# Three stacked attention layers of a graph network: in the first two, the mean squares of odd node groups move from TensorE to ScalarE and VectorE

## What is computed

```python
h, _ = jax.lax.scan(layer, x, (W, att_src, att_dst, W_e, att_edge, bias, ln_gamma, ln_beta))   # 3 layers

def layer(h_in, p):
    Wl, asl, adl, Wel, ael, bl, gl, bel = p
    h = h_in @ Wl
    a = (h @ asl)[src_f] + (h @ adl)[dst_f] + ea_f @ (Wel @ ael)
    a = jnp.where(a > 0, a, 0.2 * a)
    m = jax.ops.segment_max(a, dst_f, num_segments=n)
    ea = jnp.exp(a - m[dst_f])
    denom = jax.ops.segment_sum(ea, dst_f, num_segments=n)
    alpha = ea / denom[dst_f]
    out = jax.ops.segment_sum(h[src_f] * alpha[:, None], dst_f, num_segments=n) + bl
    mu = jnp.mean(out, axis=-1, keepdims=True)
    var = jnp.var(out, axis=-1, keepdims=True)
    out = (out - mu) * jax.lax.rsqrt(var + 1e-05) * gl + bel
    return (out, None)
```

## Time and profile before

| | us |
|---|---|
| median of 3 runs (3552.34 to 3566.22) | 3566.04 |
| the profiled execution's own time | 3538.57 |
| its span, first to last instruction | 3536.8 |
| layer 0: first transposes to last weights matmul | 2020.9 to 2433.5 |
| layer 1: the same | 2445.6 to 2858.7 |
| layer 2: first transposes to the end of the span | 2872.5 to 3536.8 |

### The profile page before, as it was taken

How to read it: one execution, slowest core, us unless ns; L and a number is a source line. 1 busy time by engine, 2 the same in 40 slices (tenths; PEclk the granted TensorE clock), 3 DMA queues, 4 the chain that set the end, 5 groups by cost and what they waited for, 6 DMA issues and landing times. The chain is left out here.

```text
span 3536.8 us, 70121 instructions
## 1 busy us (share of the span) xinstructions
PE 2946.6 (83%) x18625; PEld 2422.4 (68%) x18625; DVE 2677.1 (76%) x8976; ACT 2360.3 (67%) x6177; POOL 2132.9 (60%) x2195
## 2 busy tenths in 40 slices
PE   5997899969886997988466599997999978888893
PEld 3776777755553554545366599997999878788883
DVE  5997999985443885999677548776588778889994
ACT  3997898962322565788466567775587657877994
POOL 7777777737775774776377477403772047721677
PEclk9998999988997998999788898788999777876555
DMA  4768865445553554455477589766898568975552
GB/s 125 219 220 134 170 171 183 168 142 163 170 165 105 141 154 131 140 182 175 141 230 234 188 284 288 225 198 190 268 289 254 178 194 269 282 237 180 160 167 84
DMA packets 429483, 671.96 MB, mean 190 GB/s; under 512 B 80739, under 2 KB 167414, under 8 KB 429196
## 3 DMA queue, kind: packets, MB, share of 16 engines
q1 hardware_dynamic: 354764, 558.83, 50.2%
q0 software_dynamic: 69408, 107.46, 12.8%
q10 hardware_dynamic: 5024, 2.30, 0.3%
HBM read 376.96 MB, written 295.31 MB: 190 GB/s over the span
## 5 line engine op out<-in xcount | busy, mean ns | idle before, releaser
L662 POOL DMA_INDIRECT msgs<-t_gat,row_i x591 | 571.3, 967 | 572.4 <-POOLq L158 388.6
L2244 ACT ACTIVATE t_nnt<-t_p_nt,cxt 128x512 f32<-128x512 f32 x294 | 201.0, 684 | 307.6 <-PE t_p_nt L2124 305.1
L1769 PEld LDWEIGHTS t_p_q<-mean_col,t_nsq 128*128 128x128 f32 x2352 | 353.4, 230 | 6.4 <-issue 6.4
L1769 PE MATMUL t_p_q<-mean_col,t_nsq 128*128 128x1 f32 x2352 | 339.0, 265 | 4.5 <-ACT t_asd L2270 3.9
L2038 POOL DMA_INDIRECT out_rows<-t_x,own_i x197 | 201.4, 1022 | 209.6 <-ACT t_x L2294 154.4
L2124 PE MATMUL t_p_nt<-ident,t_nh 128*128 128x128 f32 x1176 | 223.7, 323 | 78.7 <-DMA t_nh<-t_gat 67.1
L654 POOL DMA_INDIRECT rg_ring<-t_x,row_i x197 | 197.7, 1004 | 106.0 <-issue 51.9
L654 POOL DMA_INDIRECT gc_ring<-t_x,row_i x197 | 191.1, 970 | 116.6 <-issue 59.8
L1762 PE MATMUL t_p_nh<-wx,t_nnt 128*128 128x132 f32 x1568 | 259.5, 316 | 1.2 <-DVE t_nhn L1783 1.1
L679 POOL DMA_INDIRECT dg_g_ring<-in_x,dst_i x197 | 189.9, 964 | 110.4 <-DVE g_xb L1237 55.8
L654 POOL DMA_INDIRECT g_ring<-t_h,row_i x197 | 193.9, 984 | 85.3 <-issue 59.1
(11 more groups left out here) (407 smaller groups left out, 8612.0 us busy)
## 6 DMA issues: line engine op xcount, KB each, us to landing
t_nh<-t_gat SPq DMA_DIRECT2D x294, 264.0 KB
t_gat<-t_nhn SPq DMA_DIRECT2D x196, 264.0 KB
t_x<-de_x SPq DMA_DIRECT2D x196, 256.0 KB
t_ah<-t_gat SPq DMA_DIRECT2D x150, 264.0 KB
t_x<-t_x SPq DMA_DIRECT2D x148, 256.0 KB, 4.0
t_gat<-t_ahn SPq DMA_DIRECT2D x100, 264.0 KB
t_gat<-de_h SPq DMA_DIRECT2D x98, 264.0 KB
de_x<-in_x SPq DMA_DIRECT2D x97, 256.0 KB
```

Source lines behind the costliest of these rows:

```text
L662: self.nc.gpsimd.indirect_dma_start(out=self.msgs[:, c, 0:width], out_offset=None, in_=table, in_offset=bass.IndirectOffsetOnAxis(ap=idx[: ...
L1769: last = self.nc.tensor.matmul(p_q[:, j:j + 1], sq[:, j * D:(j + 1) * D], self.mean_col[:], start=True, stop=True)
L2244: nc.scalar.activation(nnt[:, g % 2], p_nt[:], ACT.Identity, bias=bias).then_inc(act_nt, 1)
```

## The change

In layers 0 and 1, odd node groups get their mean squares in another way. ACT squares the rows as they were loaded (`nh`, 128 of the 132 columns), DVE sums the squares along a row to four numbers for each partition (`nss`) and adds a fourth extra column that the table's rows now carry, and ACT takes the root with a bias. That column is twice the product of the row with the constant `cx`, so that the square of the sum of both comes out; `cx` squared goes into the root's bias (`shift2`). The column costs no instruction in the loop, since rows were 132 wide before; filling it and `shift2` takes five more DVE instructions in the program's first phase. The four one-column matmuls (eight instructions) of an odd group go, and its ACT square of `p_nt`, in whose place stands the square of the rows at the end of the tick's node steps. Even groups, all sum groups and layer 2 keep their steps. One semaphore for all roots becomes two, one for nodes and one for sums.

SP may load over an odd group's buffer only when DVE has added the extra column. PE may turn a group over an odd group's bank when ACT has copied it, with no square to wait for.

The plan's `node_time` goes from 2.6 to 2.3, which moves the weights to later ticks: batch 0 from tick 37 to 42, batch 1 from 60 to 66, batch 2 from 83 to 91. The table grows from 116 to 124 ticks. Node groups take ticks 0 to 101 in both. Sum groups start at ticks 45, 69 and 92 before, and at 50, 75 and 100 now. Ticks in which PE has node and sum steps: 40 before (45 to 60, 69 to 84, 92 to 99), 32 now (50 to 65, 75 to 90).

```diff
-PLAN = BATCHES, (96, 190, 290), 2.6, 2.6
+PLAN = BATCHES, (96, 190, 290), 2.3, 2.6
...
+            nc.vector.scalar_tensor_tensor(out=prod[:, 0], in0=self.wx[:, :, 0:D], scalar=2.0, in1=self.cx[:, :, 0:D],
+                                           op0=ALU.mult, op1=ALU.mult).then_inc(crossed, 1)
+            nc.vector.scalar_tensor_tensor(out=prod[:, 1], in0=self.cx[:, :, 0:D], scalar=1.0 / D, in1=self.cx[:, :, 0:D],
+                                           op0=ALU.mult, op1=ALU.mult).then_inc(crossed, 1)
+            dve.wait_ge(crossed, 2)
+            nc.vector.tensor_reduce(self.wx[:, :, D + 3], prod[:, 0], AXX, ALU.add).then_inc(crossed, 1)
+            nc.vector.tensor_reduce(self.shift2[:], prod[:, 1], AXX, ALU.add).then_inc(crossed, 1)
+            dve.wait_ge(crossed, 4)
+            nc.vector.tensor_scalar(self.shift2[:], self.shift2[:], EPS, None, ALU.add).then_inc(crossed, 1)
...
+            by_rows = lambda g: not last_layer and g % 2 == 1
...
                 def nodes(i):
                     if i < DG:
                         wait(sp, pe_nt, i - UN + 1)
+                        if by_rows(i - UN):
+                            wait(sp, dve_nss, squares(i - UN, True))
                         sp.dma_start(nh[:, i % UN], self.nodes(self.th[layer], 0, i)).then_inc(narr[i % UN], 16)
...
                         pe.wait_ge(narr[g % UN], 16 * (g // UN + 1))
-                        wait(pe, act_nq, g)
+                        wait(pe, act_nt, g)
+                        if not by_rows(g - 1):
+                            wait(pe, act_nq, g)
...
-                        pe.wait_ge(act_nq, g + 1)
-                        wait(pe, act_sd, roots["n", g] - 1)
-                        self.mean_squares(p_q, nsq[:, g % 2]).then_inc(pe_nq, 1)
+                        if not by_rows(g):
+                            pe.wait_ge(act_nq, g + 1)
+                            roots_taken(pe, "n", g)
+                            self.mean_squares(p_q, nsq[:, g % 2]).then_inc(pe_nq, 1)
...
-                        nc.scalar.activation(nsq[:, g % 2], p_nt[:], ACT.Square, bias=bias).then_inc(act_nq, 1)
+                        if not by_rows(g):
+                            nc.scalar.activation(nsq[:, g % 2], p_nt[:], ACT.Square, bias=bias).then_inc(act_nq, 1)
                     if 0 <= i - 2 < DG:
                         g = i - 2
-                        act.wait_ge(pe_nq, g + 1)
                         wait(act, dve_ninv, g - 1)
-                        nc.scalar.activation(nsd[:, g % 2], p_q[:, 0:G4], ACT.Sqrt, bias=self.eps[:]).then_inc(act_sd, 1)
+                        if not by_rows(g):
+                            act.wait_ge(pe_nq, squares(g, False))
+                            nc.scalar.activation(nsd[:, g % 2], p_q[:, 0:G4], ACT.Sqrt, bias=self.eps[:]).then_inc(act_nsd, 1)
+                        else:
+                            act.wait_ge(dve_nss, squares(g, True))
+                            nc.scalar.activation(nsd[:, g % 2], nss[:, g % 2], ACT.Sqrt, bias=self.shift2[:, layer:layer + 1],
+                                                 scale=1.0 / D).then_inc(act_nsd, 1)
+                    if 0 <= i - 1 < DG and by_rows(i - 1):
+                        g = i - 1
+                        act.wait_ge(narr[g % UN], 16 * (g // UN + 1))
+                        wait(act, dve_ns, squares(g - 2, True))
+                        nc.scalar.activation(rows_of(nsq[:, g % 2]), nh[:, g % UN, :, 0:D], ACT.Square).then_inc(act_nq, 1)
...
                         self.gat_rows_out(nhn[:, g % 3], p_nh, ninv[:, g % 2]).then_inc(dve_nhn, 1)
+                    if 0 <= i - 1 < DG and by_rows(i - 1):
+                        g = i - 1
+                        dve.wait_ge(act_nq, g + 1)
+                        wait(dve, act_nsd, g - 1)
+                        nc.vector.tensor_reduce(nss[:, g % 2], rows_of(nsq[:, g % 2]), AXX, ALU.add).then_inc(dve_ns, 1)
+                        dve.wait_ge(dve_ns, squares(g, True))
+                        nc.vector.tensor_tensor(nss[:, g % 2], nss[:, g % 2], nh[:, g % UN, :, D + 3], ALU.add).then_inc(dve_nss, 1)
```

More of the change, by code:

```diff
@@ L64, in gat_plan @@
         at += node_time * (plan[-1][0] is not None) + sum_time * (i is not None)
-        if not n and i is None:
+        if not n and i is None and pieces:
             at = max(at, ready[pieces[0][0]])
@@ L282, in weights_parts @@
             sem("w_loaded"), sem("ready"), sem("folded"), sem("w_turned"), sem("kept"), sem("made"))
+        crossed = sem("crossed")
         zeroed, stored, centred, columns = sem("zeroed"), sem("stored"), sem("centred"), sem("columns")
@@ L390, in fold @@
             nc.vector.tensor_scalar(self.bet[:], self.bet[:], mean[:, 2, 0:1], None, ALU.subtract).then_inc(kept, 1)
+            dve.wait_ge(centred, 1)
+            dve.wait_ge(kept, 18)
+            nc.vector.scalar_tensor_tensor(out=prod[:, 0], in0=self.wx[:, :, 0:D], scalar=2.0, in1=self.cx[:, :, 0:D],
[7 more added lines that the diff above has]
+            nc.vector.tensor_scalar(self.shift2[:], self.shift2[:], EPS, None, ALU.add).then_inc(crossed, 1)
             dve.wait_ge(columns, 1)
@@ L1988, in phase_gat @@
             else:
[L1989 removed]
+                nss = sb("nss", [128, 2, G4]); nhn = sb("nhn", [128, 3, G4, XW]); ahn = sb("ahn", [128, 3, G4, XW])
             pe_nt, act_nt, act_nq, pe_nq, pe_nh, dve_ninv, dve_nhn = (
@@ L1993, in phase_gat @@
                 sem(n) for n in ("act_aw", "dve_aw", "pe_at", "dve_as", "act_at", "act_aq", "pe_aq", "pe_ah", "dve_ainv", "dve_ahn", "act_att"))
-            act_sd = sem("act_sd")
+            act_nsd, act_asd, dve_ns, dve_nss = (sem(n) for n in ("act_nsd", "act_asd", "dve_ns", "dve_nss"))
+            rows_of = lambda t: t.rearrange("p (c f) -> p c f", c=G4)
+            by_rows = lambda g: not last_layer and g % 2 == 1
+            squares = lambda g, rows: sum(by_rows(n) == rows for n in range(g + 1))
             pe_k, dve_k, act_k, v = sem("pe_k"), sem("dve_k"), sem("act_k"), sem("v")
@@ L2000, in phase_gat, with roots_taken @@
             msg = lambda c: self.msgs[:, c, 0:D]
-            roots = {}
+            asked = {}
             for n, a, w in plan:
                 if n is not None and 0 <= n - 2 < DG:
-                    roots["n", n - 2] = len(roots) + 1
+                    asked["n", n - 2] = (max((g for k, g in asked if k == "n"), default=-1) + 1, max((g for k, g in asked if k == "a"), default=-1) + 1)
                 if a is not None and 0 <= a - 3 < AG:
-                    roots["a", a - 3] = len(roots) + 1
+                    asked["a", a - 3] = (max((g for k, g in asked if k == "n"), default=-1) + 1, max((g for k, g in asked if k == "a"), default=-1) + 1)
+            def roots_taken(pe, kind, g):
+                nodes_asked, sums_asked = asked[kind, g]
+                while nodes_asked and by_rows(nodes_asked - 1):
+                    nodes_asked -= 1
+                wait(pe, act_nsd, nodes_asked)
+                wait(pe, act_asd, sums_asked)
             made = []
@@ L2152, in sums @@
                         pe.wait_ge(act_aq, g + 1)
-                        wait(pe, act_sd, roots["a", g] - 1)
+                        roots_taken(pe, "a", g)
                         self.mean_squares(p_q, asq[:, g % 2]).then_inc(pe_aq, 1)
@@ L2358, in nodes @@
                         g = i - 2
-                        dve.wait_ge(act_sd, roots["n", g])
+                        dve.wait_ge(act_nsd, g + 1)
                         if last_layer:
@@ L2400, in sums @@
                         g = i - 3
-                        dve.wait_ge(act_sd, roots["a", g])
+                        dve.wait_ge(act_asd, g + 1)
                         if last_layer:
```

5 lines of the change are left out of this document (2 added, 3 removed).

## The result

The changed kernel takes **3581.13 us** (median of 13 runs, 3565.84 to 3592.22) against 3552.18 us for the kernel before beside it (13 runs, 3545.76 to 3566.22). The ratio is **1.0071**, 95% interval 1.0053 to 1.0088: slower by 25 us (19 to 31; the two medians lie 29 us apart, the means 24). The forecast was 3573 us, +7, within half a percent; the range of 3540 to 3594 holds the time, but slower by more than half a percent had only a chance of 0.27.

What follows compares the result with a forecast made beforehand. TensorE was taken to bound node-only and paired ticks, VectorE sum-only ticks, with a low clock around weights batches. Two layers at +2.8 us and the first phase's +1.5 made +7.1 on 3566: 3573 us, range 3540 to 3594.

Steps and rivals of the forecast that it cites:

- Part 1: Later weights from the plan's new constant: five node-only ticks +11.2, later batches +2.2 and +6.7, end -3.4; sum +11.2 a layer.
- Part 2: Paired ticks: VectorE's added sum makes it the bound at 4.65 us a tick against 4.47; +5.2 us a layer.
- Rival (c): Paired ticks: the clock falls because TensorE no longer fills them; +197 us, price 3770, chance 0.02.
- Part 3: Node-only ticks: the wait for bank `p_nt` and SP's new wait take back TensorE's saving; 2.21 a tick, -0.7 a layer.
- rival (a): Node-only ticks: node loads land late through SP's new wait, ending slower; price 3588 us, chance 0.27.
- Part 4: Weights and first ticks: shorter odd groups -14.4, VectorE's sum delaying weights parts +4.5, clock back earlier -3, us a layer.
- Part 5: First phase: five added instructions ahead of VectorE's last one cost +1.5 us, once.
- Rival (b): Weights batches: the clock comes back to full inside them, ending faster; price 3546 us, chance 0.23.

Runs made afterwards that it cites:

- e2: The kernel before with the plan's node time at 2.3, the new placement of weights alone with no new step; 0.9987 of before.
- e6: The same kernel as e2, run again on another chip; 1.0022 of before.
- e3: The kernel before with only the first phase's additions, whose results nobody uses; 1.0006 of before; serves as before's tick table.
- e11: The changed kernel with row sums for all node groups, odd and even, of unpaired ticks, and none in paired ticks; 3539.68 us, 0.9931 of before.
- e9: The changed kernel itself, run again on the chip of e7 and e8; 1.0020 of before.
- e7: The changed kernel with row sums only for odd groups whose tick has no sum step; 0.9962 of before.
- e4: The changed kernel with five instead of four buffers for loaded node groups in layers 0 and 1; 1.0009 of before.
- e12: e7 with VectorE also making the sum and add of odd groups in paired ticks, into a tile nobody reads; 1.0044 of before.
- e1: The changed kernel with the plan's node time back at 2.6, the new steps without the new placement; 1.0022 of before.
- e5: The same kernel as e1, run again on another chip; 1.0024 of before.
- e8: The changed kernel with row sums only for odd groups whose tick also has a sum step; 1.0084 of before.
- e10: The kernel before with batches 1 and 2 due later, at 196 and 302, so no weights tick is paired; 0.9981 of before.

## Why the time lay in the range and the parts were wrong

The time came out 8 us from the forecast, and much of that is luck. The forecast stood on 3566 us, the median of three runs of the kernel before, and its thirteen runs have 3552: the base was 14 us too high. The change was forecast at +7 and is +25 (19 to 31), about 18 too low. These two errors cancel for the most part. Inside the +7, too, the parts missed by more than their sum did, in opposite directions.

**Part 1, placement, +11.2 predicted, about -5 measured.** This step failed most. The five node-only ticks are there (node-only +11 and +12 in both layers). But I costed the weights ticks at the durations that they had, low clock included, and gave them -5.5 in all; e2 and e6 show -10.6 to -13. All the rest, +16.7 by my terms (11.2 + 2.2 + 6.7 - 3.4), is then +6.6. The clock is the larger share of both misses: batches 1 and 2, when they start on lighter ticks, keep it up until part 5 or 6, and less of the low level spills into the pairs behind. At the low level a layer spends 50 us of weights ticks and 26 of pairs in e3, 39 and 9 in e2 and e6; sum-only ticks have 10 more, and the whole layer 20 less, worth some 10 of the 16 us by an estimate at half speed. Where the other 6 went wasn't worked out. On the chips where before takes 3552, the placement alone was not run. I had read the earlier trace rows as "around each batch the clock is low" and not asked which ticks took it there.

**Part 2, paired ticks, +5.2 predicted, +13.2 measured** (changed against e11, whose plan is the same; +17 in e9 against e7). The pace of 4.65 was exact. Missing were the falls of the clock. Rival (c) named them, at a chance of 0.02 and as all or nothing. In place of a total loss, TensorE loses the upper level for 3 to 10 us at a time. The row that I set against it, sum-only ticks with TensorE at 19 of 25 and PEclk 1.00, is true and no proof. The Trainium skill (TensorE: Matmul & The Clock Gate, What's actually happening) says that activity releases the throttle; this trace agrees in direction for the pairs, 22 of 25 against 25, and not in order, since e11's node-only ticks hold the clock at 17 of 25.

**Part 3, node-only ticks, -0.7 predicted, about 0 measured.** Two ticks take 4.39 instead of 4.46, as the 2.09 and 2.30 here show, so 2.195 a tick against my 2.21:

```profile
2055.01 0.60 PE L2151 MATMUL t_p_nt<-ident,t_nh 128*128 128x128 f32 x4
2056.13 1.14 PE L1774 MATMUL t_p_nh<-wx,t_nnt 128*128 128x132 f32 x8 [0.52 <-DVE t_nhn L1795]
2057.10 0.60 PE L2151 MATMUL t_p_nt<-ident,t_nh 128*128 128x128 f32 x4
...
2059.40 0.60 PE L2151 MATMUL t_p_nt<-ident,t_nh 128*128 128x128 f32 x4
```

The wait in the odd tick is for VectorE's rows out, not the one for the bank that I had named; the size was right. A few waits for loads take the rest of the gain: between 2050 and 2120 four of them, 2.0 us in all before TensorE's weight loads. That is all that is left of rival (a), and e4 finds nothing to win.

**Part 4, weights ticks, -12.9 predicted (-14.4, +4.5, -3), about 0 to +4 measured.** Ticks with the steps are 98.6 to 104.3 in e4, e7, e9 and e11, 105.3 / 106.2 in e12 and 107.4 / 101.8 in the changed kernel; with the placement alone they are 99.5 to 101.9. With the old placement the steps cost +4.5 (e1, e5 against e3). Two reasons, both in the timeline. Behind part 5 TensorE waits for VectorE's chain whatever its own speed, and what it saves it waits:

```profile
2258.51 1.82 PE L1774 MATMUL t_p_nh<-wx,t_nnt 128*128 128x132 f32 x8 [1.31 <-DVE t_nhn L1795]
2263.68 0.21 PE L2243 MATMUL t_p_w<-ident,t_bwd 32*1 32x32 f32 x1 [3.34 <-DVE t_ex L2567]
```

3.34 us here against the 1.14 of the earlier trace rows; the chain on VectorE is one of nine instructions, from 2258.40 to 2263.62. And in parts 0 to 4, where the upper clock was within reach, VectorE's sum stands ahead of the weights' parts: batch 1 of the changed kernel has 4.0, 3.7, 4.2, 4.1, 3.2 against 2.9, 3.3, 2.6, 3.4, 3.2 in e2, with 6.8 us of them at the low level where e2 has none. Much of the saving that I booked was for ticks at the low clock, which the placement by itself takes to the upper one: part 4 was worked out on the ticks of before, though part 1 changes those ticks.

**Part 5, +1.5 predicted**, +1.8 in the timeline.

**The sum.** Part 1 was 16 too high, part 2 8 and part 4 13 to 17 too low for each layer, which is why the sum is nearer than its parts; a layer is +8.5 (the mean of 11.8 and 5.1) where I had +2.8, and two of them are +17 of the 25. The other 8 lie outside the two layers; the two profiled executions, 31.3 apart, have 14.4 there: 1.8 in the first phase, 7.8 in phases whose code is the same and 4.8 in layer 2. That more than the 1.8 belongs to the change isn't shown: in one comparison on one chip layer 0 began at 2941 us of e9, 2960 of e7 and 2964 of e8, three kernels with the same code up to there. Nor is it ruled out: outside the condition of e1 to e10, the three traces with the new first phase begin layer 0 at 2030.5 (changed), 2029.7 (e11) and 2034.4 (e12), and the one without it at 2020.9. For the same reason, and by the slower pairs, the batches of weights began at 2129, 2233 and 2351 us and not near 2118, 2215 and 2330. Rival (b), the clock back inside the weights, came true in part, by the placement and not by the steps.
